# A four-layer network on one core: readout of a selective scan moved partly to TensorE and ScalarE, more banks at the start of two local attentions, a bias moved in two attentions, and a reordered head

## Time and profile before

| | us |
| --- | --- |
| three plain runs, median | 1950.32 (1950.08 to 1950.96) |
| the profiled execution | 1951.72 |
| its span, first to last instruction | 1949.7 |
| mean granted TensorE clock | 0.898 |

### The profile page before, as it was taken

The page is one execution under the profiler, slowest core; times in us unless marked ns, Lnnn a source line. Parts: engine busy times, 40 slices in busy tenths (PEclk is TensorE's granted clock), DMA queues, the critical chain, the costliest instruction groups (busy, mean ns, idle before and its releaser), DMA issues. The chain is left out here.

```text
span 1949.7 us, 31910 instructions
## 1 busy us (share of the span) xinstructions
PE 1535.3 (79%) x10847; PEld 1085.7 (56%) x10847; DVE 1057.3 (54%) x2489; ACT 878.1 (45%) x1937; POOL 646.2 (33%) x723
## 2 busy tenths in 40 slices
PE   3579976799776577774839998899987699879986
PEld 2356664466563123232827776777766577746654
DVE  5366543665376999995034553355534422545443
ACT  5345543455446666661424443534433233335540
POOL 1487514776132576661330000100002421511111
PEclk8699987899897799997869998999988799979995
DMA  8200000000000000005124000000000011300000
GB/s 225 80 7 17 12 6 2 12 12 17 6 1 0 1 0 0 0 0 108 49 58 158 1 0 1 1 1 1 1 1 1 28 49 28 39 2 2 2 2 22
DMA packets 54016, 46.54 MB, mean 24 GB/s; under 512 B 24536, under 2 KB 40328, under 8 KB 53896
## 3 DMA queue, kind: packets, MB, share of 16 engines
q1 hardware_dynamic: 50104, 38.65, 7.3%
q0 software_dynamic: 3072, 6.30, 1.6%
q10 hardware_dynamic: 720, 0.02, 0.0%
HBM read 31.25 MB, written 9.44 MB: 21 GB/s over the span
## 5 line engine op out<-in xcount | busy, mean ns | idle before, releaser
L1279 POOL TENSOR_TENSOR inject<-delta_x,b_rows 128x512 f32<-128x512 f32 x128 | 162.2, 1275 | 84.7 <-ACT b_rows L1413 64.5
L1486 DVE TENSOR_TENSOR_SCAN state<-bank,inject 128x512 f32<-128x512 f32 x128 | 155.6, 1215 | 4.0 <-POOL inject L1279 3.8
L1322 PE MATMUL bank<-x_work,tabs 128*128 128x512 f32 x256 | 138.9, 626 | 16.3 <-DVE y L1499 14.7
L1418 ACT ACTIVATE bank<-delta,a_neg 128x255 f32 (+1 forms) x256 | 111.5, 468 | 40.9 <-DVE state L1486 39.6
L1900 POOL TENSOR_TENSOR ve<-mv,eps 128x1 f32<-128x1 f32 x32 | 6.1, 190 | 368.9 <-DVE mv L2034 368.9
L584 POOL TENSOR_TENSOR rotated<-rot_cos,rot_sin 128x512 f32<-128x512 f32 x64 | 80.9, 1268 | 71.3 <-DVE rot_sin L862 71.3
L2911 DVE TENSOR_REDUCE top<-bank 128x2 f32<-128x512 f32 (+1 forms) x96 | 61.9, 686 | 72.1 <-PE bank L2653 51.3
L1997 ACT ACTIVATE Z<-bank 128x512 f32<-128x512 f32 x64 | 34.7, 595 | 140.2 <-PE bank L1954 140.2
L590 POOL TENSOR_TENSOR inv_norm<-sum_sq,neghalf 128x16 f32<-128x16 f32 x32 | 93.7, 2929 | 2.7
L1977 ACT ACTIVATE U<-bank 128x512 f32<-128x512 f32 x128 | 72.7, 591 | 48.2 <-PE bank L1921 48.2
L859 DVE TENSOR_TENSOR rot_cos<-bank,rope 128x512 f32<-128x512 f32 x64 | 43.9, 685 | 92.8 <-ACT squares L780 74.9
(11 more groups left out here) (538 smaller groups left out, 4199.6 us busy)
## 6 DMA issues: line engine op xcount, KB each, us to landing
v<-v SPq DMA_DIRECT2D x32, 130.0 KB, 2.3
slots<-zero SPq DMA_DIRECT2D x10, 256.0 KB, 4.1
moe_w<-in_L_ffn_rg_dram SPq DMA_DIRECT2D x1, 2048.0 KB, 9.4
moe_w<-in_L_ffn_ru_dram SPq DMA_DIRECT2D x1, 2048.0 KB, 14.5
wqkv<-in_L_ffn_wqkv_dram SPq DMA_DIRECT2D x2, 768.0 KB
slots_out<-y SPq DMA_DIRECT2D x1, 1280.0 KB, 8.0
x_tok<-in_L_attn_x_dram SPq DMA_DIRECT2D x4, 256.0 KB, 5.6
slots_out<-y SPq DMA_DIRECT2D x8, 128.0 KB, 1.8
```

Of the source, the lines that this page charges most:

```text
L1279: pool.tensor_tensor(dB[:, k % R, :, :], dx[:, :, bass.ds(i * L, L)], both(b_rows[:, k % R, :]), ALU.mult)\
L1322: pe.matmul(sum_bank[:, :], ident, flat(hc[:, m % R, :, :]), start=(m == 0), stop=(m % NS == NS - 1))\
L1418: act.activation(dA[k % 2][:, c, 1:L], delta[:, c, bass.ds(i * L + 1, L - 1)], ACT.Exp, scale=a_neg[:, c, k:k + 1])\
L1486: dve.tensor_tensor_scan(flat(h[:, m % R, :, :]), flat(dA[m % 2]), flat(dB[:, m % R, :, :]), 0.0, ALU.mult, ALU.add)\
```

## The change

It joins edits in five stages.

- **Recurrence:** ACT waits for `a_param` only, and for the gates' biases later; DVE keeps x instead of ACT; PE adds the residual into the banks as soon as the gate has been read (`residual`), so `turn_h` has four matmuls instead of eight; POOL instead of DVE multiplies with the root; `running` has 256 instead of 2048 columns.
- **Local attention, ahead of the loop:** batch 0 is projected into four banks (`own = X + O`), and batch 1 as soon as these come free; turning, values and copies of batch 0 use S; DVE makes half of the tables, all four adds and the last two scalings of batch 0; POOL takes the power on 8 columns at a time. The loop itself is kept, but for one wait of the first `mix`.
- **Inputs of the scan:** unrolled, two sets of four banks, two buffers; ACT does the padded copy and the first tap.
- **Scan:** written out without loops. The rows of B go to DRAM and come back by DMA as broadcasts over 128 partitions, four states at a time in four buffers. The decay has three banks. Every even step is read out by token: PE transposes the state, ACT scales it by the column of C (a scalar for each token) and PE adds it back transposed. Odd steps are read out as before, with the row of C made by one fp32 product over 33 rows. The skip term is a product with a diagonal on PE. `step` of groups 1 to 3 comes inside batch 0.
- **Attention of layer 2:** the bias is broadcast once into `pb_rows`, and DVE adds it while it takes bank 3 to SBUF.

The core of the diff (each "..." leaves lines out):

```diff
@@ stage_recurrence
+                for g in range(G):
+                    pool.wait_ge(s.root.sem, s.root.at(0, g + 1))
+                    pool.wait_ge(s.weighed.sem, s.weighed.at(0, g + 1))
+                    pool.tensor_tensor(gx[:, cols(g)], gx[:, cols(g)], a2[:, cols(g)], ALU.mult).then_inc(s.scaled.sem, 1)
...
+                def residual(g):
+                    pe.wait_ge(s.gate_x.sem, s.gate_x.at(0, g + 1))
+                    for t in range(TPG):
+                        pe.matmul(bank[g][:, t * P:(t + 1) * P], net.xT[:, tok(g, t)], ident, start=(t == 0), stop=False)
...
-                act.wait_ge(par_in, 48)
+                act.wait_ge(par_in, 16)
...
+                def keep_x(g):
+                    dve.wait_ge(s.x_ps.sem, s.x_ps.at(0, g + 1))
+                    dve.tensor_copy(net.xT[:, cols(g)], bank[g][:, :]).then_inc(s.xT_in.sem, 1)
@@ stage_local_attention, pool
+                for m in range(4):
+                    first_norms(m)
+                    if m == 1:
+                        for k in range(2):
...
+                            pool.tensor_tensor(r, r, rn[:, k, :].unsqueeze(2).to_broadcast([P, LH, LDH]), ALU.mult).then_inc(s.roped.sem, 1)
@@ stage_local_attention, pe
+                own = X + O
                 for m in range(4):
+                    project(0, 0, m, own[m])
+                for m in range(3):
+                    pe.wait_ge(s.sind.sem, s.sind.at(0, m + 1))
+                    project(1, 1, m, own[m])
+                turn(0, 0, 0, S)
+                turn(0, 0, 1, S)
+                pe.wait_ge(s.sind.sem, s.sind.at(0, 4))
+                project(1, 1, 3, own[3])
+                highest(0, 0)
...
@@ stage_local_attention, vector
+                rotate(0, 0)
+                rotate(0, 1)
+                add_parts(0)
+                add_parts(1)
+                rotate(0, 2, O)
+                rotate(0, 3, O)
+                add_parts(2)
+                add_parts(3)
+                scale(2)
+                scale(3)
+                highest(0, 0)
+                rotate(1, 0)
+                highest(0, 1)
                 split_top(0)
+                rotate(1, 1)
+                rotate(1, 2, O)
+                rotate(1, 3, O)
@@ stage_scan, sync
+                for q in range(CHUNKS):
+                    i, k = q * CH // NS, q * CH % NS
...
+                    if q >= 4:
+                        sp.wait_ge(s.inject.sem, s.inject.at(0, CH * (q - 3)))
+                    sp.dma_start(b_all[:, q % 4, :, :], b_dram[k:k + CH, i * L:(i + 1) * L].partition_broadcast(P)).then_inc(b_in[q % 4], 16)
@@ stage_scan, tensor
+                def turn(n):
...
+                    for t in range(TPB):
+                        for c in range(2):
+                            last = pe.transpose(turn_bank(n)[:, t * 2 * P + c * P:t * 2 * P + (c + 1) * P], h[:, n % R, c, tok(t)], ident)
+                def c_row(n):
...
+                    pe.matmul(c_bank[:, 0:L], ident[0:XP, 1 + NS + k:2 + NS + k].to_broadcast([XP, P]), ssm[:, seq(n)], start=True, stop=True).then_inc(s.c_ps.sem, 1)
+                def add(n):
+                    if by_token(n):
...
+                                last = pe.matmul(sum_bank[:, c * L + t * P:c * L + (t + 1) * P], hcT[:, j % RT, t, c * P:(c + 1) * P], ident,
+                                                 start=(k == 0 and t == 0 and c == 0), stop=False)
+                    else:
+                        last = pe.matmul(sum_bank[:, :], ident, flat(hc[:, j % R, :, :]), start=False, stop=(k == NS - 1))
...
+                for n in range(LAST + LAG):
+                    if 1 <= n <= LAST and by_token(n - 1):
+                        turn(n - 1)
+                    if n < LAST and not by_token(n):
+                        c_row(n)
+                    if n >= LAG:
+                        add(n - LAG)
@@ stage_scan, scalar
+                    for t in range(TPB):
+                        last = act.activation(hcT[:, j % RT, t, :], turn_bank(n)[:, t * 2 * P:(t + 1) * 2 * P], ACT.Copy, scale=c_cols[:, TPB * i + t, k:k + 1])
@@ stage_scan, vector
+                for n in range(LAST + 1):
+                    i, k = n // NS, n % NS
+                    if 1 <= i < B and k == 4:
+                        gate(i - 1)
+                    if n < LAST:
+                        scan(n)
+                    if n >= 1 and not by_token(n - 1):
+                        read(n - 1)
+                    if i == 0 and k in (2, 6, 10):
+                        step(k // 4 + 1)
@@ stage_mha
+                pe.matmul(bank[3][:, 0:D], net.tab("ones")[0:1, :], w.pb[:, :], start=True, stop=True).then_inc(s.pb_ps.sem, 1)
+                pe.wait_ge(s.pb_rows.sem, s.pb_rows.at(0, 1))
...
-                    pe.wait_ge(s.xn_ready.sem, s.xn_ready.at(i, j))
+                    pe.wait_ge(s.y_sum.sem, s.y_sum.at(i, j))
...
-                    pe.matmul(bank[3][:, 0:D], net.tab("ones")[0:1, :], w.pb[:, :], start=False, stop=False)
...
-                            dve.bn_stats(st[:, :], bank[3][:, 0:D]).then_inc(s.stats.sem, 1)
+                            dve.tensor_tensor(y_sb[:, j % 2, :], bank[3][:, 0:D], pb_rows[:, :], ALU.add).then_inc(s.y_sum.sem, 1)
+                            dve.wait_ge(s.y_sum.sem, s.y_sum.at(i, j + 1))
+                            dve.bn_stats(st[:, :], y_sb[:, j % 2, :]).then_inc(s.stats.sem, 1)
```

More of the change, by code:

```diff
@@ L329, in _ @@
                     gate_x(g)
+                for g in range(G):
+                    residual(g)
                 turn_h(0)
@@ L1183, in _ @@
+                pad(0)
+                for i in range(B):
+                    gates(i)
+                    if i + 1 < B:
+                        pad(i + 1)
+                    conv(i)
             @block.vector
@@ L1311, in _, with columns @@
-                steps(groups - 1)
-                pe.wait_ge(s.parts.sem, s.parts.at(0, groups))
-                pe.wait_ge(s.sel.sem, s.sel.at(0, 2))
+                def columns(first, end):
+                    for t in range(first, end):
+                        for c in range(2):
+                            last = pe.matmul(bank[6][:, t * NS:(t + 1) * NS], xc[:, c, tok(t)], net.w_xproj[:, c, 1 + NS:XP], start=(c == 0), stop=(c == 1))
+                    return last
+                project_in(0)
@@ L1350, in _ @@
-                batch(0, False)
-                with pe.Fori(1, B) as i:
-                    batch(i, True)
-                for m in range(NS - LAG, NS):
-                    add(B - 1, m)
+                            pe.matmul(y_bank[:, tok(t)], y2[:, c, tok(t)], net.w_out[:, c, :], start=(c == 0), stop=False)
+                        last = pe.matmul(y_bank[:, tok(t)], net.xT[:, i * L + t * P:i * L + (t + 1) * P], ident, start=False, stop=True)
+                    last.then_inc(s.y_ps.sem, 1)
@@ L1427, in _, with decay @@
-                batch(0, False)
-                with act.Fori(1, B) as i:
-                    batch(i, True)
-                keep(B - 1)
+                def decay(n):
+                    i, k = n // NS, n % NS
+                    if k == 0 and i % 2 == 0:
+                        act.wait_ge(s.delta.sem, s.delta.at(0, i // 2 + 1))
+                    if n >= RD:
+                        act.wait_ge(s.state.sem, s.state.at(0, n - RD + 1))
+                    for c in range(2):
+                        last = act.activation(dA[n % RD][:, c, 1:L], delta[:, c, i * L + 1:(i + 1) * L], ACT.Exp, scale=a_neg[:, c, k:k + 1])
+                    last.then_inc(s.decay.sem, 1)
@@ new lines, in scale @@
+                def scale(n):
+                    i, k, j = n // NS, n % NS, n // 2
+                    act.wait_ge(s.turned.sem, s.turned.at(0, j + 1))
+                    if j >= RT:
+                        act.wait_ge(s.added.sem, s.added.at(0, 2 * (j - RT) + 1))
+                    for t in range(TPB):
+                        last = act.activation(hcT[:, j % RT, t, :], turn_bank(n)[:, t * 2 * P:(t + 1) * 2 * P], ACT.Copy, scale=c_cols[:, TPB * i + t, k:k + 1])
+                    last.then_inc(s.scaled.sem, 1)
@@ L1432, in _ @@
+                update(B - 2)
+                update(B - 1)
             @block.vector
```

646 lines of the change are left out of this document (315 added, 331 removed).

## The result

The kernel after takes 1893.37 us (median of 4 runs, 1890.14 to 1896.02) against 1950.64 (1950.08 to 1952.65) beside it: ratio 0.9704, 95% interval 0.9687 to 0.9721. The prediction was 1875.5, within 1852 to 1898. So 57 us came where 74.8 were forecast, and the reading starts with the question which stage kept the other 18. The profiled execution of after took 1893.07, span 1891.3.

What follows compares the result with a forecast made beforehand. It took DVE to bound the scan loop and PE the attentions and local attentions; scan -20.8, attentions -19.0, local attentions -26.4, recurrence -4.6 and scan inputs -4.0 sum to -74.8, from 1950.3 to 1875.5 us, range 1852 to 1898.

Steps and rivals of the forecast that it cites:

- PE takes over the loop at 3.0 a pair: Scan loop: changes of row number around the row of C make PE the bound, 27.4 us a batch instead of 30.2.
- the first rival: Scan loop: row of C costs no change of rows, DVE stays the bound; scan gives 35.6, time 1867 or 1861; chance 0.25.
- the first scan comes 1.6 earlier: Ahead of the scan loop: without the bf16 splitting but with columns of C on PE, first scan 1.6 us earlier.
- fourth rival: Scan: PE falls to 1.2 GHz for longer than now, adding some 10 us, time 1886; chance 0.1.
- the +2.6: Scan, batch 0: three groups of step sizes move into it, so it takes 30.0 us instead of 27.4.
- behind the last scan -1.5: End of the scan stage: one readout and the skip terms go, saving 1.5 us.
- The local attentions: First batches of both local attentions: second turn of batch 1 comes 13.2 us earlier in each, 26.4 together.
- the second rival: Local attentions: POOL or waits between batches eat the gain, only 5.4 per stage stays, time 1891; chance 0.15.
- The two attentions: Masked and unmasked attention: bias matmul and two changes of row number go, 0.61 us an item, 19.0 together.
- The inputs of the scan: Stage making the scan's inputs: copy and first tap go to ACT, 3.2 to 3.4 a batch, saving 4.0 us.
- The recurrence: Head of the kernel: last copy at 55.0 instead of 60.9, but SP's zero writes until 56.25 limit the gain to 4.6.
- The third rival: Scan loop: slow DMA of the rows of B makes POOL wait; at 50 GB/s, time 1991; chance 0.02.

Runs made afterwards that it cites:

- e2: Kernel after with the product for the row of C over 128 rows instead of 33: ratio 0.9621 to the kernel before.
- e3: Kernel after with the matmuls for the columns of C behind the last step sizes on PE instead of in front: ratio 0.9639 to the kernel before.
- e5: Kernel after with row of C over 128 rows, columns of C behind the step sizes, exponential of `a_log` at the stage's head: ratio 0.9533 to the kernel before.
- e10: Kernel after with the three scan edits of e5 and the DVE adds of e8: 1934.11 us, ratio 0.9532 to the kernel before.
- third edit: Part of e5 against the kernel after: exponential of `a_log` and its sign moved to the head of the scan stage; not timed alone.
- e4: Kernel after with all four groups of step sizes ahead of the first scan, instead of three inside batch 0: ratio 0.9731 to the kernel before.
- e8: Kernel after with DVE instead of POOL adding batch 1's second pair of parts in the local attentions: ratio 0.9683 to the kernel before.
- e7: Kernel after with both attentions' bias back on PE, as a product over 128 rows, without DVE's add: ratio 0.9741 to the kernel before.
- e6: e5 with all four groups of step sizes ahead of the first scan: ratio 0.9550 to the kernel before.
- e11: e10 with all four groups of step sizes ahead of the first scan: 1928.55 us, ratio 0.9524 to the kernel before.

## Why the prediction was right or wrong

**Right: PE takes over the loop at 3.0 a pair, because the row of C changes the number of rows.** It was the choice between 2.6 and 3.0 that the prediction made from the one-row and 32-row products of the attention. The pair is 3.01, the batch 27.6 against the 27.4 forecast, and with 128 rows in place of 33 the 0.4 goes and DVE is the bound at 25.5. Its sign, a gap of 0.2 at both sides of the row of C, did not come in that form: the gaps are 0.09 ahead of it, 0.19 behind it and 0.11 behind the add. Without the price, the first rival's 24.8 plus 0.5 a batch nearly comes out (e2).

**Wrong: "the first scan comes 1.6 earlier".** It came 10.4 later, a miss of 12.0 us, and the largest. The step was "PE gets 32 matmuls for the columns of C (7.0 at 0.22) in front of the last step sizes; followed along the chain of ACT". Two things in it failed. The chain that ends last in the prologue is PE's and not ACT's: ACT waits 12.5 and 6.3 us for it. And the matmuls were priced at 2.4 GHz: at a granted clock of 0.65 they cost 10.5, and the others around them 6.3 more. Moving them off that chain gave all 17 back in e3. In e5 and e10, where the clock stayed low, it gave 14 together with the third edit. The stage of the kernel before shows no such work, so its clock of 0.92 between 611 and 627 could not be carried over.

**Too small: the ends of the loop.** Batch 0 took 31.9 instead of 30.0 (by the count of scans, sixteen between 620.40 and 652.3): the three moved `delta` instructions took 1.85, 2.05 and 2.05 instead of 1.22, and the first pairs ran at 1.2 GHz. Batch 1 took 31.7 instead of 27.4, at a granted clock of 0.50 from 650 to 655 and 0.62 to 660. PE had stood 2.65 us behind the third group of steps just before. The prediction had a fall of the clock as its fourth rival, at 10 us and a chance of 0.1; it named the loop as its place, where in fact the prologue paid 6.3 and the first two batches up to 5. e2, e3 and e4, which all reach the first gate of the loop 5.0, 4.9 and 8.4 earlier, show that it is not a price of the loop as such.

The forecast for this part was also added up wrongly. Seven batches at 2.8 to 2.9 less are some 20, and batch 0, at 30.0 against 30.2, is not longer than before; the +2.6 compares it with the new batches and takes back a gain that had not been counted. By its own numbers the prediction should have had some 20 for the loop instead of 17.7, and about 1873 for the whole, so that the loop's 12.4 missed by 8 and not by 5.

**Wrong: behind the last scan -1.5, measured +0.9.** PE is the bound and still has its last steps to add when DVE ends, so the gate waits 4.04 for it. With PE off the bound (e2) the end is 11.4, 0.7 shorter than before.

**The local attentions: 23.2 instead of 26.4.** The path was followed right for most of its length: last scaled part 18.8 behind the opening (forecast 17.9), top_row 27.1 (27.8), POOL's adds of batch 1 done at 34.0 (35.3), first turn of batch 1 15.8 earlier than before (the sign had 13), second turn ended at 40.4 (39.1). The step that is missing is the wait behind the adds: DVE's sum of squares of batch 2 waits 1.87 for POOL's power of batch 1, and the turn behind it ran at the low clock, 1.12 instead of 0.66. It is the second rival's mechanism in small, POOL holding up the first batches. Taking two adds from POOL moved the turn with the power (e8). It took 1.6 us a stage, not the 7.8 at which the rival was priced.

**The two attentions: 18.1 instead of 19.0.** The item is 0.67 shorter, not 0.61, in both of them (10.98 to 10.31, 11.70 to 11.03); why the stretch as a whole gained less than 32 of these is not settled. e7 confirms the split of the price.

**The inputs of the scan: 7.9 instead of 4.0.** The term was mis-sized by its bound: PE was taken at the low clock, 3.4 a batch, and ACT at 3.0. ACT sets the period, with 2.66 and no gap between its instructions, and PE's eight records take 2.00, at a granted clock of 1.00 from 550 to 555.

**The recurrence: 5.3 instead of 4.6.** The compute ended at 55.1 (forecast 55.0), SyncE 0.8 earlier than before, so the two waits now end within 0.3 us of each other.

**The third rival, the DMA of the rows of B, did not show:** 66 GB/s over the loop, a chunk lands in 8.3 us at the median, and POOL's idle time is put down to DVE.

**How much of the total is luck.** The scan missed its term by 19.7 us, with a cause in the prologue that no rival names. That 1893 still lies within 1852 to 1898 is not to the forecast's credit: the upper end had been set to hold the second rival, whose 1891 the measured time happens to meet while its mechanism took 3.2 us in all, and 3.9 more from the inputs of the scan and 3.0 from stages that nobody changed cover part of the miss.

## What to carry to other kernels

When work moves ahead of a loop, follow every engine's list there, not only the one that was last before, and price PE's part at the clock that the stage is granted: here small products forecast at 7 us cost 10.5, and the low clock cost the products around them 6.3 more. A product over few rows between products over 128 cost 0.4 us beyond its columns in two stages of this kernel; making it over 128 rows (padded with zeros in e2), which costs nothing in columns, or putting it elsewhere, was worth more than most of the edits of the change. And work whose result is needed late belongs behind the work that the next engine waits for.

## What was not expected of the hardware

- The granted clock of TensorE fell to 0.50 while PE had no gap at all: from 590 to 600 in e3 PE was busy the whole time, with products over 16 columns only. The Trainium skill (TensorE: Matmul & The Clock Gate, Part 1) calls the gate's low state that of an idle array; in this stretch the instruction rows show no idle time, and the products that stood between these in the kernel after ran at 1.2 GHz too (3.78 for four records instead of 1.98).
- The same sixteen products at the head of the same stage took 16.4 us in e3 and e6, 20.0 in e11 and 21.6 in e5 and e10, at granted clocks around 0.66 where they were slow and 1.00 where they were fast.
- DVE's products with two operands in SBUF took 2.17 to 2.28 instead of 1.22 while POOL multiplied (e4). The Trainium skill (SBUF — State Buffer, "SBUF: two separate sides") describes a lock on a port pair that such instructions share with POOL; the rows agree, with up to 1.06 us a time.
- Stages that no kernel here changes took 65 us (top-2 experts) and 7 to 12 us (switch experts) more on three chips than on the first.
